# Moving each stage's loads and first products into the norm ahead of it, with a token-major capacity count and rope tables made during the input load

## The reference, cut to what matters

```python
x = _layernorm(x + _L0_attn_ref(x, ...))    # windows of 32 tokens
x = _layernorm(x + _L0_ffn_ref(x, ...))     # 16 experts, 4 of a token, sigmoid scores in groups, and a shared one
x = _layernorm(x + _L1_attn_ref(x, ...))    # 8 heads with directions of 3 numbers
x = _layernorm(x + _L1_ffn_ref(x, ...))     # 8 experts, 2 of a token, capacity 640
x = _layernorm(x + _L2_attn_ref(x, ...))    # 8 heads of 128 with rope
x = _layernorm(x + _L2_ffn_ref(x, ...))     # rmsnorm, 16 heads of 64 with rope, rmsnorm, 31 experts
x = _layernorm(x + _L3_attn_ref(x, ...))    # rmsnorm, gated recurrence, rmsnorm, gated mlp
x = _layernorm(x + _L3_ffn_ref(x, ...))     # 8 experts and a shared one; logits with a hidden layer
```

```python
mask = jax.nn.one_hot(jnp.swapaxes(topi, 0, 1), N_EXP, dtype=jnp.int32)
rank = jnp.cumsum(mask.reshape(TOP_K * N, N_EXP), axis=0).reshape(TOP_K, N, N_EXP) - 1
mask = mask * (rank < capacity)

return shared + routed + an + attn_out      # attn_out = ctx @ o_w + o_b + xn, an = rmsnorm(attn_out)
```

## Time and profile before

| | |
|---|---|
| time, median of 3 runs (lowest, highest) | 2051.99 us (2046.13, 2059.99) |
| profiled execution, its time / its span | 2053.46 us / 2051.7 us |
| PE busy / DVE / ACT / POOL, share of the span | 83% / 55% / 55% / 36% |
| DMA | 120.28 MB, mean 59 GB/s |

### The profile page before, as it was taken

How to read it: one execution, slowest core, us unless ns; L and a number is a source line. 1 busy time by engine, 2 the same in 40 slices (tenths; PEclk the granted TensorE clock), 3 DMA queues, 4 the chain that set the end, 5 groups by cost and what they waited for, 6 DMA issues and landing times. The chain is left out here.

```text
span 2051.7 us, 27897 instructions
## 1 busy us (share of the span) xinstructions
PE 1695.6 (83%) x8871; PEld 1087.0 (53%) x8888; DVE 1137.3 (55%) x2224; ACT 1118.9 (55%) x2343; POOL 734.2 (36%) x665
## 2 busy tenths in 40 slices
PE   5659778862999789999939999999959998757797
PEld 3337534331888456666515555555527885312685
DVE  4936564517666355555435555555546885542475
ACT  2324443441887445555446655555527887653596
POOL 1214320020333256666315555555313442000363
PEclk8869865775999899999979999999968999978898
DMA  1008100000211222222121111111007661000330
GB/s 32 1 13 183 33 4 1 1 21 22 97 62 52 77 52 57 62 61 54 31 74 45 42 43 42 41 42 42 23 12 256 210 223 45 19 8 19 103 115 24
DMA packets 52778, 120.28 MB, mean 59 GB/s; under 512 B 12724, under 2 KB 21660, under 8 KB 45468
## 3 DMA queue, kind: packets, MB, share of 16 engines
q1 hardware_dynamic: 52636, 118.55, 19.9%
HBM read 82.86 MB, written 2.10 MB: 41 GB/s over the span
## 5 line engine op out<-in xcount | busy, mean ns | idle before, releaser
L750 DVE TENSOR_TENSOR e_lo<-psum,e_hi 128x512 fp32r<-128x512 f32 x296 | 203.0, 686 | 87.0 <-ACT psum L715 87.0
L1343 ACT ACTIVATE h_probs<-psum,h_nmax 128x512 f32<-128x512 f32 (+3 forms) x256 | 132.6, 523 | 133.2 <-DVE h_nmax L1421 78.5
L673 PE MATMUL psum<-f_x_hi,f_w_hi 128*128 128x512 f32 x400 | 159.8, 399 | 38.6 <-PEq L843 36.1
L1421 DVE TENSOR_REDUCE h_nmax<-psum 128x1 f32<-128x512 f32 (+3 forms) x256 | 113.6, 486 | 119.3 <-PE psum L1232 119.3
L674 PE MATMUL psum<-f_x_hi,f_w_lo 128*128 128x512 f32 x400 | 159.0, 398 | 0.0
L675 PE MATMUL psum<-f_x_lo,f_w_hi 128*128 128x512 f32 x400 | 159.0, 397 | 0.0
L1158 POOL TENSOR_TENSOR h_swapped<-h_swapped,a2f_tables 128x512 f32<-128x512 f32 x64 | 81.7, 1276 | 200.4 <-DMA h_swapped<-h_raw 200.4
L715 ACT ACTIVATE psum<-psum,f_b 128x512 f32<-128x512 f32 x200 | 131.9, 660 | 30.1 <-PE psum L675 29.9
L692 PE MATMUL psum<-e_lo,f_w_hi 128*128 128x512 f32 x364 | 142.2, 391 | 1.9 <-POOL e_lo L641 0.9
L689 PE MATMUL psum<-e_hi,f_w_hi 128*128 128x512 f32 x364 | 142.2, 391 | 0.0
L690 PE MATMUL psum<-e_hi,f_w_lo 128*128 128x512 f32 x364 | 141.9, 390 | 0.0
(11 more groups left out here) (425 smaller groups left out, 4135.6 us busy)
## 6 DMA issues: line engine op xcount, KB each, us to landing
e_gate<-gates SPq DMA_DIRECT2D x46, 1024.0 KB, 4.7
a_swapped<-a_raw SPq DMA_DIRECT2D x128, 128.0 KB, 2.3
h_swapped<-h_raw SPq DMA_DIRECT2D x256, 64.0 KB, 2.0
e_gate<-gates SPq DMA_DIRECT2D x16, 512.0 KB, 7.1
f_w<-in_l_experts SPq DMA_DIRECT2D x8, 512.0 KB, 5.6
f_w<-in_l_experts SPq DMA_DIRECT2D x32, 128.0 KB, 4.7
e_gate<-gates SPq DMA_DIRECT2D x12, 256.0 KB, 3.9
f_w<-in_l_experts SPq DMA_DIRECT2D x9, 256.0 KB, 4.9
```

What stands on the lines that cost most here:

```text
L673: nc.tensor.matmul(to, w_h, ex.x_hi[:, cols(b)], start=True, stop=False, skip_group_check=True)
L750: nc.vector.tensor_tensor(lo[:, n % PLACES, :], whole, hi[:, n % PLACES, :].bitcast(F32), ALU.subtract).then_inc(lo_dve, 1)
L1343: nc.scalar.activation(probs[:, j % 4, 0:(q + 1) * P], ring[j % RING][:, 0:(q + 1) * P], ACT.Exp, bias=nmax[:, j % 8:j % 8 + 1], accum_out ...
L1421: nc.vector.tensor_reduce(nmax[:, j % 8:j % 8 + 1], ring[j % RING][:, 0:(q + 1) * P], AX.X, ALU.max, negate=True).then_inc(max_ready, 1)
```

## The change

What it does, by parts.

1. `norm` takes an object `ahead` with code for SP, PE and DVE that runs inside the norm's block: SP issues the next stage's loads at the start of the norm, and PE's first products of the next stage stand behind the norm's own. `RouterFront` (r0, r1, r2) holds loads, the experts' first weights and the logit products, a chunk at a time as DVE finishes it; for r3 it holds the loads alone. `RopeFront` holds the weights of a2 (in n1f) and h2 (in n2a, ahead of g1), `DirectionFront` all of stage a1w (in n0f; two DVE copies stand between the third and fourth chunk of the norm), `HawkFront` the loads of rc and gm (in n2f), `WindowFront` those of l0a (in the load block), `StoreFront` the whole of the store (in n3f).
2. To make room for it a norm uses two banks for the means of squares instead of four and PE's order is centre 0, centre 1, mean 0, centre 2, mean 1, centre 3, mean 2, mean 3.
3. The rope tables of h2 are made in the load block into memory kept to the end; stage rt is gone. The input is loaded in four pieces behind the identity, and ACT instead of DVE copies the transposed x.
4. r1 counts token-major: two products of 128 x 256 with a triangular and an all-ones matrix (`c_counts`), eight scans of 32 elements over the tiles' totals, and six small DVE operations; its gates are 32 columns a tile, as in the other routers. The 8 x 2048 operations are gone.
5. The copy to `gates_t` is four of 32 x 512, DVE and ACT in turn. The two additions in f2 are gone: the residual of r2 is three products a chunk (`an`, `core.sum`, `core.x`), 24 passes.
6. In direction attention PE spreads the sums in step 1 and turns the maxima in step 2, ACT's and DVE's parts following.
7. A `recycle` is added behind h2.

```diff
@@ norm
-        xc = [core.psum[:, b, :] for b in range(4)]
-        var = [core.psum[:, 4 + b, :] for b in range(4)]
+        xc = [core.psum[:, 4 + b, :] for b in range(4)]
+        var = [core.psum[:, 2 + b, :] for b in range(2)]
         with nc.Block() as block:
+            @block.sync
+            def _(sp):
+                ahead.sync(sp)
+
             @block.tensor
             def _(pe):
-                if center:
-                    for b in range(B):
+                def centre(b):
+                    if center and b < B:
                         nc.tensor.matmul(xc[b], core.center_w[:], src[:, cols(b)], start=True, stop=True).then_inc(centered, 1)
+
+                centre(0)
+                centre(1)
                 for b in range(B):
                     pe.wait_ge(squared, b + 1)
-                    nc.tensor.matmul(var[b], core.mean_w[:], sq[:, b % 2, :], start=True, stop=True).then_inc(var_ready, 1)
+                    if b >= 2:
+                        pe.wait_ge(ln_ready, b - 1)
+                    nc.tensor.matmul(var[b % 2], core.mean_w[:], sq[:, b % 2, :], start=True, stop=True).then_inc(var_ready, 1)
+                    centre(b + 2)
+                ahead.tensor(pe, out_ready)
@@ RouterFront
+    def sync(self, sp):
+        for to, of in self.loads:
+            sp.dma_start(to, of).then_inc(self.loaded, 16)
+        for s in range(self.ex.ring):
+            self.ex.load_weights(sp, s)
+
+    def tensor(self, pe, out_ready):
+        if self.hw is None:
+            pe.wait_ge(self.loaded, 16 * len(self.loads))
+            for b in range(B):
+                pe.wait_ge(out_ready, b + 1)
+                for t in range(b * QT, (b + 1) * QT):
+                    last = self.core.nc.tensor.matmul(self.logits[:, t, :], self.x[:, t * P:(t + 1) * P], self.rw[:, 0, :], start=True, stop=True)
+            last.then_inc(self.logits_ready, 1)
@@ DirectionFront, in n0f
+    def tensor(self, pe, out_ready):
+        core = self.core
+        pe.wait_ge(self.loaded, 4 * 16)
+        for k in range(2):
+            core.nc.tensor.matmul(core.psum[:, k, 0:2 * P], self.w3[:, k, :], self.spread[:], start=True, stop=True).then_inc(self.wide_psum, 1)
@@ StoreFront, in n3f
+    def tensor(self, pe, out_ready):
+        nc, core = self.core.nc, self.core
+        for b in range(B):
+            pe.wait_ge(out_ready, b + 1)
+            if b >= 2:
+                pe.wait_ge(self.tiles_out, b - 1)
+            for q in range(QT):
+                last = nc.tensor.transpose(core.psum[:, b % 2, q * P:(q + 1) * P], core.x[:, (b * QT + q) * P:(b * QT + q + 1) * P], core.ident[:])
+            last.then_inc(self.tiles_ready, 1)
@@ Experts.residual
-                self.core.nc.tensor.matmul(self.acc[b], self.core.ident[:], self.resid[:, cols(b)], start=True, stop=True, skip_group_check=True)
+                for k, of in enumerate(self.resid):
+                    self.core.nc.tensor.matmul(self.acc[b], self.core.ident[:], of[:, cols(b)], start=k == 0, stop=k == len(self.resid) - 1,
+                                               skip_group_check=True)
@@ router, r1 on DVE (the 8 x 2048 operations that go are listed by the orders below)
+                    dve.wait_ge(counted, 2)
+                    for e in range(E):
+                        last = nc.vector.tensor_tensor_scan(upto[:, :, :, e].rearrange("p k t -> p (k t)"), front.table[:, 1, 0:2 * NT],
+                                                            totals[:, :, :, e].rearrange("p k t -> p (k t)"), 0.0, ALU.mult, ALU.add)
+                    step(last)
+                    step(nc.vector.tensor_tensor(upto[:], upto[:], totals, ALU.subtract))
+                    step(nc.vector.tensor_tensor(upto[:], upto[:], within, ALU.add))
+                    step(nc.vector.scalar_tensor_tensor(chosen[:], upto[:], float(capacity), chosen[:], ALU.is_le, ALU.mult))
+                    step(nc.vector.tensor_tensor(first, first, wide(small[:, :, 2:3], E), ALU.mult))
+                    step(nc.vector.tensor_tensor(second, second, wide(small[:, :, 3:4], E), ALU.mult))
+                    nc.vector.tensor_tensor(g_tm[:, :, 0:E], first, second, ALU.add).then_inc(gates_ready, 1)
+
+                for b in range(0, B, 2):
+                    dve.wait_ge(gates_t_psum, b + 1)
+                    nc.vector.tensor_copy(gates_t[:, cols(b)], core.psum[0:W, b, :]).then_inc(copied, 1)
@@ direction_attention, the tensor engine's steps
-                    if k == 1 and U + 1 < n_units:
+                    if k == 1 and U >= 1:
+                        spread_sums(U - 1, m_read)
+                        m_read = ln_ready, U
+                    if k == 2 and U + 1 < n_units:
                         max_rows(U + 1, m_read)
                         m_read = q_ready, U + 2
-                    if k == 2 and U >= 1:
-                        spread_sums(U - 1, m_read)
-                        m_read = ln_ready, U
@@ build_program
-        load_start(core)
         window_attention(core)
-        post_norm(core, "n0a")
         ffn0(core)
-        post_norm(core, "n0f")
         attn1(core)
```

576 lines of the change are left out of this document (298 added, 278 removed).

## The result

| | before | after |
|---|---|---|
| time, median (lowest, highest; runs) | 2051.2 us (2046.13, 2059.99; 4) | 1917.68 us (1911.42, 1923.81; 4) |
| ratio of the two, 95% interval | | 0.9339 (0.9302 to 0.9377) |
| profiled execution, its time / its span | 2053.46 / 2051.7 us | 1913.05 / 1910.9 us |
| mean granted clock of PE | 0.886 | 0.931 |

The kernel is 133.5 us faster by the medians. The profiled execution of after is one of its two shorter ones (1911.4 and 1913.1 us; the others took 1922.3 and 1923.8), so its span moved by more, 140.8 us. The page of after says how that divides: sections 1 and 2, busy us with the share of the span and the number of instructions, and the granted clock in forty slices.

A forecast was written before the change was run, and what follows sets the result against it. The prediction saw PE held up by norm chains, loads after norms and two stretches without matrix work. Its terms summed to -114 us: 1939.5 against the profiled 2053.5, 1938 against the median, range 1915 to 1964.

The forecast's parts named there:

- r1: Router r1, norm's end to e1: token-major count and moved loads and logits cut 55.0 us to about 24; -31 us.
- rival B: Direction attention: shorter idle stretches let it begin at full clock, 22 us saved at most; total 1918 us; chance 0.11.
- direction attention: Direction attention: PE no longer waits 13.7 us for the maxima, something comes late in its place; -11 us, bounds 5 and 16.
- Rival A: PE's clock eats part of the gain, moved work leaving PE longer at 1.2 GHz; total 1957 us; chance 0.18.
- r2: Router r2: additions, load and logits go, but the residual's 24 passes at 0.82 us make PE late next; -12 us.
- r0: Router r0: scores come 6.7 us sooner with logits in the norm, and the copy in pieces saves 1.3; -8 us.
- Norms: Eight centred norms: first mean of squares comes behind the second centring product, 1.7 us gained each; -13.6 us.
- rope tables and recycle: Stage rt ahead of h2 goes, -12.4 us, its chain hidden in the load block; the recycle behind h2 costs +0.6.
- starts and store: Starts of rc (-3.5), gm (-4.6) and r3 (-6.2) follow the barrier alone, and the store gains 2; together -16.3 us.
- Rope attentions: h2 and a2: second group of weights no longer late, ending ACT's 2.86 us wait; -2.5 us each, -5 together.
- D: Prefetch saves less than the waits show, since early loads meet other transfers or a barrier; total 1978 us; chance 0.05.
- C: Slower than before: a long stage of experts stays at 1.2 GHz behind a router; 2102 us at 400 passes; chance 0.03.

The follow-up runs named there:

- b_att_max: Kernel before with only the turning of the maxima in direction attention moved to step 2, behind the spread sums; 2048.1 us, ratio 0.9975.
- b_att: Kernel before with only the whole new order of direction attention (sums in step 1, maxima in step 2); 2024.59 us, ratio 0.9856.
- a_att_old: Kernel after with the old order of direction attention put back (maxima in step 1, sums in step 2); 1940.15 us, ratio to before 0.9448.
- a_resid_dve: Kernel after with r2's two residual additions back on DVE, in a block between g2 and the router; 1928.2 us, ratio to before 0.9405.
- a_cap_old: Kernel after with before's masks, scans along 2048 tokens and wide gates in r1; 1946.08 us, ratio to before 0.95.
- a_pool_late: Kernel after with POOL's splitting of x and first weights in every router held until DVE's first MAX8; 1921.77 us, ratio to before 0.9385.
- a_pool_norm: Kernel after with POOL's splitting of x held until DVE's first MAX8 and the first weights split in the norm's block; 1916.41 us, ratio to before 0.9363.
- b_norm: Kernel before with only the norm's new product order and its two banks for the means of squares; 2039.58 us, ratio 0.9938.
- b_pad: Kernel before with unused memory that puts e1's tiles at the addresses they have in after; 2057.59 us, ratio 1.0023.
- a_best: Kernel after with a_pool_norm's edit and 3008 unused bytes that move e1's tiles back into line; 1911.66 us, ratio to before 0.9321.

## Why the prediction was right, and where it was not

The direction and the range (1915 to 1964) held, and of the larger terms r1's. The single number was 20 us too high: the sum had -114 where the span moved by -140.8 and the medians by -133.5. The measured 1917.7 lies outside the forecast's own range (1927 to 1950), on the number of rival B, so that the wide range was kept in part by luck. The order of the terms did not hold: direction attention, sixth in size in the sum, gave the most. Most of the difference is that one term.

**Direction attention (-11, was -30.6): the step that failed.** It took 11 of the 13.7 us of the wait for `a_nparts` as the prize, and held the clock for "a little", 2.3 us at the bound of 16. In the profiles PE's idle time in the stage fell by 6.1 us and its busy time by 24.5, with the clock at 0.94 for 0.70. `b_att_max` takes the same wait away, and the stage is 1.5 us shorter; what the whole new order gains above all is the full clock. Why this order brings it stays open. Rival B had the size of it (1918, and 22 us in this stage at most by the clock) but the wrong cause, shorter idle time ahead of the stage: `b_att` has before's start and gets the 30 us, `a_att_old` has after's and does not. So the number of B came true by luck, through a mechanism that it did not have. Rival A did not come: the mean clock rose from 0.886 to 0.931.

**r2 (-12, was -21.6).** Mis-sized by the price of the residual. "At 6.55 / 8 = 0.82 each" was that of a pass at the lower clock, from a place where PE had just waited 13.33 us for a load; in after it comes from work. The passes took 0.43 each, 10.5 us instead of 19.6, and ended at E + 12.0, not at E + 18.7. So "PE, not DVE, is late next" was wrong too: the gates were ready at E + 14, as forecast, and PE waits 1.96 us for DVE. The forecast stopped at the store of the gates; up to there the stretch is 18.1 us shorter and not 12, and the bias products behind it, 7.16 to 3.67 us, are the other 3.5. `a_resid_dve` shows that the clock which the residual keeps up is the reason for these.

**r1 (-31, was -29.6).** Right, and for the reason given; `a_cap_old` sets the count at 24.8. Two sizes in it were off and partly cancel: eight scans took 1.00 us, not 2.5, and the choice of experts 11.5, not 8.5, of which 2.2 are a subtraction that took 2.45 us beside POOL.

**r0 (-8, was -4.3).** The scores came sooner as forecast. What was not asked is who stands beside DVE once its work starts sooner: POOL, which cost between 2.0 us (`a_pool_late`) and 2.9 (`a_pool_norm`). The 0.8 that is left of the difference is as much as r0 varies between kernels that don't differ in it (28.0 to 28.8).

**Norms (-13.6, was -17.1).** The term was mis-sized: by 1.98 us of ACT's wait only the time up to the first logarithm was counted. That gave 14.4 us of the 17.1; the other 2.6 came behind it, where the forecast had the chunks "at ACT's pace as before". Three norms (n1f, n2f, n3a) take 8.66 us, 2.4 to 3.0 less. `b_norm` has 16.4 of it with nothing else changed, so the moved work is not seen to help or to harm a norm.

**a1w (-5.3, was -6.9), rope tables and recycle (-11.8, about -13.0), starts and store (-16.3, was -17.8)** were right to 2 us each. DVE waited 0.38 us for the wide products where 1.5 had been expected, and the load block became 0.9 us shorter with the tables in it, so nothing of the sines was seen. **Rope attentions (-5)** is not seen in h2 (-0.1), and in a2 it is within what that stage varies. ACT's wait of 2.86 us for the second weights is gone in both, but the second group of products starts only 1.1 us sooner behind the first in h2 and 1.3 in a2, and nothing of it is left at the stage's end; h2's first product still waits 5.84 us, for DVE's splitting of the first group (L1572).

**Experts (0, was +5.0).** Nothing in the diff touches them. e1's +3.9 is the place of its tiles (`b_pad`, `a_best`); e0's +1.2 lies within what that stage takes over all kernels here, 84.6 to 86.3 us.

**D and C** did not happen: no load ends a first wait of these stages, and windows of 80 to 130 us inside e0 to e3 have a granted clock of 0.96 to 1.00, as in before.

## What to carry to other kernels

A wait of PE in a stage that runs at half clock can't be priced by its length alone: read the granted clock beside it, and look at what an order does to the clock by running it, for here the same products took 108 or 138 us. Work of PE that has room under another engine's chain can pay even if it is more than needed: 24 passes in place of 8 cost nothing in r2 and left PE at the full clock for what stands behind them. When a step is moved forward, list what the other engines do at its new time, for here POOL beside DVE took 2 to 3 us of the 8 that r0 was to gain. When tiles move, measure a stage whose code did not change. And before a row of a profile is called a gain, look at how much that stretch varies between kernels that don't differ in it.

## What the runs showed of the hardware that was not expected

- PE can be busy for 14.66 of 15 us at a granted clock of 0.50, in a stage whose mean is 0.66 over 137 us (`b_att_max`); another order of the same products brings it to 1.00 in some 20 us (`b_att`, after).
- Products of 128x512 at the full clock take 389 ns in the mean, or 391 to 399 by their group, by where their tiles lie (1088 bytes modulo 4096 here), with nothing else changed; 16 rounds of six take 21.76 or 22.35 us.
- A DVE addition or subtraction took 0.23 us alone and 1.04 beside a POOL operation at 64 elements, 0.29 and 2.45 at 128.
- Eight scans of 32 elements with one input in PSUM took 1.00 us together, 0.125 each; two scans of 2048 took 4.4 us each.
